# Loading x by eights of batches into a ring of three eights

## What is computed

```python
x = x + einsum('bct,bcd->bdt', x, L0_weights[itok_B_1_198])   # 128 x 128 matrix of 200
x = x + einsum('bct,bcd->bdt', x, L1_weights[itok_B_0_7])     # 128 x 128 matrix of 8
      + bias[itok_B_0_7][:, :, None]
```

## Time and profile before

| | us |
|---|---|
| median of three runs | 342.63 |
| the profiled execution | 343.0 |
| its span, first to last instruction | 341.2 |
| TensorE busy with matmuls | 272.9 (80%) |
| VectorE, ScalarE, GpSimd busy | 126.3, 97.0, 65.8 |
| bytes moved | 140.8 MB, 413 GB/s over the span |
| share of the 16 DMA engines' time, SP's queue | 98.7% |

### The profile page before, as it was taken

How to read it: one execution, slowest core, us unless ns; L and a number is a source line. 1 busy time by engine, 2 the same in 40 slices (tenths; PEclk the granted TensorE clock), 3 DMA queues, 4 the chain that set the end, 5 groups by cost and what they waited for, 6 DMA issues and landing times.

```text
span 341.2 us, 4867 instructions
## 1 busy us (share of the span) xinstructions
PE 272.9 (80%) x774; PEld 131.8 (39%) x774; DVE 126.3 (37%) x202; ACT 97.0 (28%) x135; POOL 65.8 (19%) x249
## 2 busy tenths in 40 slices
PE   1799997678777798786997977889697987978980
PEld 1355443334333354343443433444343443434430
DVE  3145543343333334243442433434243432424440
ACT  1033352232322224132241324313143321323330
POOL 2400311131122211222111222121222111222000
PEclk9999999999999979799897999979799997989996
DMA  7999999999999999999999999999999999999993
GB/s 304 417 409 396 422 430 419 413 423 421 432 434 423 426 422 414 431 424 423 427 427 423 431 430 426 427 421 426 433 426 430 427 429 426 425 426 424 413 387 137
DMA packets 24058, 140.80 MB, mean 413 GB/s; under 512 B 2673, under 2 KB 14322, under 8 KB 15474
## 3 DMA queue, kind: packets, MB, share of 16 engines
q1 hardware_dynamic: 23760, 140.20, 98.7%
q10 hardware_dynamic: 290, 0.53, 0.4%
HBM read 76.03 MB, written 67.11 MB: 419 GB/s over the span
## 4 chain that ended last, share of the span: by engine, by line
DMA 61%; SPq 16%; PE 13%; issue 7%; ACT 0%; DVE 0%; DVEq 0%
DMA out<-xy 54%; PE y_ps L310 11%; SPq L129 9%; SPq L123 5%; DMA xy<-x 4%; DMA w_home<-w_t 2%; PE m_ps L291 2%; SPq L148 2%; ACT xy L406 0%; SPq L162 0%; SPq L151 0%; SPq L203 0%; SPq L156 0%; PE home_ps L324 0%; SPq L176 0%
## 5 line engine op out<-in xcount | busy, mean ns | idle before, releaser
L310 PE MATMUL y_ps<-xy,m_sb 128*128 128x512 f32 x512 | 251.4, 627 | 49.2 <-DMA xy<-x 48.2
L310 PEld LDWEIGHTS y_ps<-xy,m_sb 128*128 128x128 f32 x512 | 94.6, 200 | 155.1 <-issue 155.1
L406 ACT ACTIVATE xy<-y_ps,j_pick 128x512 f32<-128x512 f32 x128 | 88.0, 687 | 227.4 <-PE y_ps L310 227.4
L382 DVE TENSOR_SCALAR xy<-y_ps,j_pick 128x512 f32<-128x512 f32 x128 | 96.1, 751 | 147.9 <-PE y_ps L310 147.9
L242 POOL COPY w_pick<-w_home 128x128 f32 x112 | 33.2, 296 | 238.3 <-issue 238.3
L291 PEld LDWEIGHTS m_ps<-j_pick,w_pick 128*128 128x128 f32 x224 | 35.7, 200 | 30.2 <-issue 29.7
L374 DVE TENSOR_TENSOR m_sb<-m_ps,j_pick 128x256 f32<-128x256 f32 x64 | 27.2, 425 | 47.7 <-PE m_ps L291 46.1
L291 PE MATMUL m_ps<-j_pick,w_pick 128*128 128x128 f32 x224 | 34.9, 279 | 0.0
L244 POOL COPY j_pick<-j_all 128x129 f32 x112 | 33.4, 298 | 0.1
L291 PE MATMUL m_ps<-j_pick,w_home 128*128 128x128 f32 x32 | 5.9, 315 | 6.6 <-DMA w_home<-w_t 6.6
L406 ACT ACT_TABLE_LOAD x7 | 9.0, 1283 | 7.5 <-POOL j_pick L256 7.4
(11 more groups left out here) (16 smaller groups left out, 2.8 us busy)
## 6 DMA issues: line engine op xcount, KB each, us to landing
xy<-x SPq DMA_DIRECT2D x30, 2048.0 KB, 15.1
out<-xy SPq DMA_DIRECT2D x29, 2048.0 KB, 15.0
w_home<-w_t SPq DMA_DIRECT2D x128, 64.0 KB
out<-xy SPq DMA_DIRECT2D x5, 1024.0 KB, 9.7
xy<-x SPq DMA_DIRECT2D x3, 1024.0 KB, 7.7
xy<-x SPq DMA_DIRECT2D x4, 256.0 KB, 13.4
j_all<-w_bias SPq DMA_DIRECT2D x1, 516.0 KB, 3.4
out<-xy SPq DMA_DIRECT2D x2, 256.0 KB, 4.7
```

What stands on the lines that cost most here:

```text
L310: nc.tensor.matmul(y_ps[:, b % YB, h, :], m_sb[:, s, k, :], xy[:, s, k, half(h)], start=True, stop=True).then_inc(y_ready, 1)
L382: nc.vector.tensor_scalar(xy[:, s, k, half(0)], y_ps[:, b % YB, 0, :], j_pick[:, s, k, D:D + 1], None, ALU.add).then_inc(left_out[b % YB], 1)
L406: nc.scalar.activation(xy[:, s, k, half(1)], y_ps[:, b % YB, 1, :], ACT.Identity, bias=j_pick[:, s, k, D:D + 1]).then_inc(right_out[b % YB ...
```

## The change

x (the input alone) is laid out by *eights* of batches: 128 rows of 32 KB, 4.19 MB. `xy` is a ring of three eights (12 pairs instead of 8), and there are five rounds of it and a sixteenth eight at the end. An eight is loaded by one DMA; the first is loaded as two pairs and a quad, the last as a quad, a pair and four halves of a batch. Stores stay quads. `w0_pick`, `j_pick` and `m_sb` shrink to rings of four pairs (PB), and `pick` waits for the results of the pair four behind (`wait_free`), no longer for a store. In SP's order, a step stores a quad, waits for both quads of the eight three behind, loads the eight in its place, and stores the next quad:

```diff
-    RING = 8
...
+    EIGHT = EB // PAIR
+    EIGHTS = 3
+    RING = EIGHTS * EIGHT
...
+    PB = 4
+    BY_PAIR = 3
+    END = EIGHT - 1
...
+            def load_eight(r, e):
+                sp.dma_start(slots(e * EIGHT, EIGHT), eight_of_x(r, e)).then_inc(x_loaded[e], 16)
...
+            def wait_stored(r, e):
+                for q in range(2 * e, 2 * e + 2):
+                    sp.wait_ge(stored[q], stored_once(r, q))
+
+            def next_of(r, e):
+                return (r, e + 1) if e + 1 < EIGHTS else (r + 1, 0)
+
+            def step(r, e):
+
+                behind = next_of(r - 1, e)
+                load_w0_of(r, 2 * e)
+                store_quad(behind[0], 2 * behind[1])
+                load_w0_of(r, 2 * e + 1)
+                wait_stored(r, e)
+                load_eight(r, e)
+                store_quad(behind[0], 2 * behind[1] + 1)
...
             for s in range(QUAD):
-                load_pair(0, s, pair_loaded[s])
+                load_part(0, s, 1, pair_loaded[s])
             sp.wait_ge(cond_loaded, 16)
-            for q in range(QUADS):
-                load_w0_first(q)
-                if q < QUADS - 1:
-                    load_quad(0, q + 1)
+            load_w0_first(0)
+            load_part(0, QUAD, QUAD, quad_loaded)
+            load_w0_first(1)
+            for e in range(1, EIGHTS):
+                load_eight(0, e)
+                load_w0_first(2 * e)
+                load_w0_first(2 * e + 1)
...
             sp.wait_ge(home_ready, 4)
...
+            load_w0_of(1, 0)
+            for s in range(EIGHT):
+                store_pair(0, s)
+            load_w0_of(1, 1)
+            for s in range(EIGHT, EIGHT + QUAD):
+                store_pair(0, s)
+            wait_stored(1, 0)
+            load_eight(1, 0)
             store_quad(0, 3)
...
+            for e in range(1, EIGHTS):
+                step(1, e)
+            with sp.Fori(2, ROUNDS) as r:
+                for e in range(EIGHTS):
+                    step(r, e)
+
...
+            load_w0_of(ROUNDS, 0)
+            store_quad(ROUNDS - 1, 2)
+            load_w0_of(ROUNDS, 1)
+            wait_stored(ROUNDS, 0)
+            load_part(NE - 1, 0, QUAD, last_quad_loaded)
+            load_part(NE - 1, QUAD, 1, last_pair_loaded)
             for k in range(PAIR):
                 for h in range(2):
-                    sp.dma_start(xy[:, LAST, k, half(h)], x[NQ - 1, :, QB - PAIR + k, half(h)])\
+                    sp.dma_start(xy[:, END, k, half(h)], x[NE - 1, :, EB - PAIR + k, half(h)])\
                       .then_inc(last_x_loaded[2 * k + h], 16)
-            for q in range(1, QUADS - 1):
+            for q in range(3, QUADS):
                 store_quad(ROUNDS - 1, q)
-            store_pair(ROUNDS - 1, LAST - 1)
+            store_quad(ROUNDS, 0)
+            store_pair(ROUNDS, END - 1)
...
+            def wait_free(r, s):
+
+                n, behind = (r, s - PB) if s >= PB else (r - 1, s - PB + RING)
+                for k in range(PAIR):
+                    b = behind * PAIR + k
+                    pool.wait_ge(left_out[b % YB], n * (ROUND_B // YB) + (b // YB + 1))
+                    pool.wait_ge(right_out[b % YB], n * (ROUND_B // YB) + (b // YB + 1))
...
-                    pool.wait_ge(stored[s // QUAD], stored_once(r, s // QUAD))
                     pick(r, s)
+            for s in range(EIGHT):
+                pick(ROUNDS, s)
```

More of the change, by code:

```diff
@@ L12, in conditioned_residual_kernel @@
 def conditioned_residual_kernel(nc, x, cond, w0_t, w1_bias, out):
-    NQ, C, QB, T = x.shape
-    B = NQ * QB
+    NE, C, EB, T = x.shape
+    NQ, _, QB, _ = out.shape
+    B = NE * EB
     N0, _, D = w0_t.shape
@@ L145, in load_w0, with load_part @@
                     load_one(b + k, s + k // PAIR, words[2 * k], words[2 * k + 1])
[L147 to L151, removed]
+            def load_part(n, s, pairs, loaded):
+                sp.dma_start(slots(s, pairs), part_of_x(n, s, pairs)).then_inc(loaded, 16)
+            def load_eight(r, e):
+                sp.dma_start(slots(e * EIGHT, EIGHT), eight_of_x(r, e)).then_inc(x_loaded[e], 16)
             def wait_out(r, s):
@@ L193, in _ @@
[L193 to L199, removed]
-            store_quad(0, 3)
[L201 to L209, removed]
@@ L253, in pick_first @@
                     skip_runtime_bounds_check_because="each word is checked against its own range below")
+                if s >= PB:
+                    wait_free(0, s)
                 for k in range(PAIR):
@@ L298, in results @@
                 if k == 0:
-                    if first and s < QUAD:
+                    if last:
+                        if s < QUAD:
+                            pe.wait_ge(last_quad_loaded, 16)
+                        elif s < END:
+                            pe.wait_ge(last_pair_loaded, 16)
+                    elif first and s < QUAD:
                         pe.wait_ge(pair_loaded[s], 16)
-                    elif not last:
-                        pe.wait_ge(x_loaded[s // QUAD], r * 16 + (16 if s >= QUAD else 0))
+                    elif first and s < EIGHT:
+                        pe.wait_ge(quad_loaded, 16)
+                    else:
+                        pe.wait_ge(x_loaded[s // EIGHT], r * 16 + (16 if s >= EIGHT else 0))
                     pe.wait_ge(m_ready[s % MB], r * (RING // MB) + (s // MB + 1))
                 for h in range(2):
-                    if last:
+                    if last and s == END:
                         pe.wait_ge(last_x_loaded[2 * k + h], 16)
@@ L337, in _ @@
                     results(r, s - 1, 1)
+            results(ROUNDS - 1, LAST, 0)
+            product(ROUNDS, 0)
+            results(ROUNDS - 1, LAST, 1)
+            for s in range(1, EIGHT):
+                results(ROUNDS, s - 1, 0, last=True)
+                product(ROUNDS, s)
+                results(ROUNDS, s - 1, 1, last=True)
             for k in range(PAIR):
-                results(ROUNDS - 1, LAST, k, last=True)
+                results(ROUNDS, END, k, last=True)
         @block.vector
@@ L391, in _ @@
                     left(r, s, 1)
[L392 to L395, removed]
-                left(ROUNDS - 1, s, 1)
+            for s in range(EIGHT):
+                left(ROUNDS, s, 0)
+                if s < END:
+                    sum_m(ROUNDS, s + 1)
+                left(ROUNDS, s, 1)
         @block.scalar
```

101 lines of the change are left out of this document (48 added, 53 removed).

## The result

The changed kernel takes 355.06 us (354.21 to 358.53, five runs) beside 342.96 of the kernel before on the same chip: 1.037 of it [1.035, 1.040], 12 us more. The forecast was 342.5, no change, with 345.0 as the upper end.

A forecast was written before the change was run, and what follows sets the result against it. Transfers on full DMA engines, ending with the slowest, were taken to bound the kernel. Terms -1.0 + 0.2 + 0.7 = -0.1 us against the profiled 343.0 us, 0.4 above the median, gave 342.5 us, range 340.3 to 345.0.

The forecast's parts named there:

- What bounds the kernel: Whole kernel: DMA engines are full, the slowest sets the end, and only holes on it cost time.
- Part 1: Large loads of x: 32 KB rows mean fewer packets, 7 to 13 ns saved for each large one; -1.0 us.
- rival C: Loads of x: the chip cuts 32 KB rows into two packets, nothing gained but small packets; 343.4 us, chance 0.10.
- Part 2: Unconditional first round of W0 loads: grows from 16 to 24 batches, one repeated matrix more loaded; +0.2 us.
- Part 3: Start: full queue holds SP at W0 loads behind the third eight, first store late, a hole on all engines; +0.7 us.
- Rival B: Start: queue full before SP's last unconditional W0 loads are in, hole of 3.0 us; 344.8 us, chance 0.14.
- Part 4: Loop: 4.9 us behind the awaited store suffices for the slowest engine; engines ahead may run dry; cost 0.
- My tells: Signs to look for: loop shares a little under 1.00; against it, low shares in every step with TensorE waiting longer.
- `wait_free` and the rings: Picks in the loop: the pair four behind was done some 11 us before it is needed; cost 0.
- Computing stays covered: Loop: TensorE needs 17.5 of 20.6 us for two quads, so computing stays hidden behind transfers; cost 0.
- Rival D: Loads of x: reads spaced by 32 KB are slower, +2.9 us and no packet gain; 346.3 us, chance 0.07.
- Tail: End: three quads' stores (14.7 us) behind the last loads close the hole at 324 us, which was free; cost 0.

The follow-up runs named there:

- e2: Changed kernel with the second store of each step issued before the wait and the load, rows still 32 KB: 348.86 us, 1.019.
- e3: Changed kernel with e2's store order, and each eight loaded by two transfers with rows of 16 KB: 347.60 us, 1.015.
- e6: Kernel before, SP's loop written out, each load also waiting until the previous load landed, so one quad's store (4.9 us) stands behind: 369.06 us, 1.080.
- e8: Kernel before with only the change's small rings of picks and products (four pairs): 343.14 us, 1.0017.
- e5: e3 with a semaphore for each quad of x, so TensorE may start at an eight's first quad: 347.08 us, 1.014.
- e4: Kernel before, own order and ring, with x laid out by eights: 16 KB rows spaced by 32 KB: 342.84 us, 1.0008.
- e10: The control with 32 more waits on a long-reached semaphore in each of SP's unrolled steps: 349.14 us, 1.019.
- e11: Kernel before with 32 more waits on a long-reached semaphore in each step of SP's loop, not unrolled: 343.64 us, 1.003.
- the control: Kernel before with SP's loop only written out (unrolled), no wait added: 344.64 us, 1.007.
- e9: Changed kernel's rings and layout, but each step stores a quad, waits for the quad six behind and loads one quad: 346.75 us, 1.013.

## Why the prediction was wrong

**What bounds the kernel.** Right: the transfers do, before and after. Right too that the end belongs to the slowest engine. Wrong was what I took from it, that only a hole on that engine costs anything.

**Part 1, rows of 32 KB: right in mechanism.** 23760 - 22032 = 1728 packets fewer in SP's queue: 1792 large and 224 small ones less, as forecast, and against them 144 for the W0 load and 144 for a quad that is now stored as two pairs. A 32 KB row is one packet (rival C is out); undisturbed it takes 1213 ns against twice 611, 9 ns saved, where I took 7 to 13. But the microsecond never reached the time, since slow packets cover it; and where part of these were gone, in e2 and e3, the kernel with large rows was the longer one by 1.3 us.

**Part 2, one more W0 load: right**, 0.06 MB more.

**Part 3, the start: right in mechanism, too large in size.** SP was held by the full queue as described (after, start us, us, line, transfers):

```profile
16.93 6.05 SPq L165 DMA_DIRECT2D xy<-x  x1
23.48 13.80 SPq L143 DMA_DIRECT2D w_home<-w_t  x12
37.47 3.09 SPq L180 DMA_DIRECT2D out<-xy  x4
```

All twelve W0 loads, however, were in the queue (23.48 + 13.80 = 37.3 us) before the last engine was through with the third eight, at 38.1 us, and the store came at once. I had put two or so of them behind that moment. The windows there:

```profile
36.00:37.00 1.00, 1.00 (x6) 0.60 (x5) 0.42 (x1) 0.66 (x1) 0.07 (x1) 1.00 0.44 137
37.00:38.00 1.00, 1.00 (x4) 0.44 (x3) 0.72 (x1) 0.00 (x0) 0.00 (x0) 1.00 1.15 300
```

0.4 us at most, against 0.7. Rival B, 3.0 us, is out.

**Part 4, the loop: this is the step that failed.** I wrote that 4.9 - 2.2 "leaves at least 2.7 us on the slowest engine, so nothing is lost there. Engines that are up to 5 us ahead of it do run dry, and can afford it". The 5 us between the engines were right, and the 2.7 us were near (by the trace 3.2 to 4.1). What is false is that nothing is lost and that the engines ahead can afford it. With 4.9 us behind the awaited store the packets of a load take up to 3.1 us instead of 1.2, behind its start on the engines that ran dry, and at its end on all 16, so that the slowest engine is held too. The idle time itself is small, some 2 us for each engine over the whole run; the slow packets are some 15 us. The price of this term was 0; e6 gives it by itself as 1.0 us a step, so 12 us.

My tells failed with it. I looked for "shares of a little under 1.00", and for "low shares in every step" as the sign against me. Shares stay at 1.00, because a slow packet counts as busy. GB/s is the column that falls. Two other signs were there: TensorE waited longer (48.2 us before, 53.7 after), and the last engine stood 2 us nearer to the first (a lag of 3.6 us at 300 us, 5.8 before). The prediction's last words even name the fault, that 4.9 us is too little to stand behind the store, but gave it neither a price nor a chance.

**`wait_free` and the rings: right** within 0.6 us (e8). **Computing stays covered:** not quite. As long as a full eight must land, results are late enough to empty a longer queue (e3 has slow packets in the loop, e5 none).

**Rival D, the spacing: out** (e4, 1.0008). The rule of the Trainium skill beside it (DMA: Bandwidth & Descriptors, Latency and other measured facts) speaks of pitches from 512 KiB up; 32 KB here cost nothing, and no run here shows a larger one.

**Tail.** As forecast there is no hole at 324 us (1.01, 389 GB/s), and that was worth nothing.

**The sum.** -1.0 + 0.2 + 0.0 to 0.4 for the first three parts, of which the -1.0 is not seen in any time, and 12 us for the fourth. No rival held it: each rival was a price of a part in which I saw a cost, and part 4 had been closed at 0.

**What stays open.** That the short queue costs the 12 us is shown: e6 makes the same loss for each step in the kernel before, by it alone, and e2, e3 and e5 take it away in the loop, step by step. Why packets are slow then was not found; the trace shows when and on how many engines, not what they wait for. That engines which ran dry start together is not enough to explain it: slow packets also come at the ends of loads, and at loads for which no engine had run dry (51 and 94 us after, 238 to 250 us in e10). The missing proof is a run in which only some of the engines restart. That instruction packets set the last engine back is shown by the steps in e10, e11 and the control. They don't account for all of e9's 4.3 us: its packets at 69.9, 98.4, 114.5 and 151.0 us come with steps of 0.4, 0.1, 0.6 and 1.0 us, the large one at 86.2 us with none, and the rest of its lag grows between packets, twice as fast as before (0.2 and 0.1 us in 10). The cause of that is open. In e5 the lag grows as far, to 8.9 us at 298 us, so a part of its 4.5 us can be the same and not the tail.

## What to carry to other kernels

Where a DMA queue bounds a kernel, compare what stands behind the awaited transfer with the distance between the first and the last of the 16 engines plus the start of a load; where it was shorter, each step cost about 1 us on all engines, although none of them seemed idle. Making the transfer twice as large, without putting more behind the awaited store, halved this reserve here, from 9.8 to 4.9 us. Read GB/s beside the share: a busy share of 1.00 says nothing of how fast the packets go.

## What the runs showed of the hardware

- A short queue costs more than the idle time in it: 1.0 us a step with 4.9 us behind the awaited store, nothing measurable with 9.8 us as long as the lag stayed under 7.6 us, at busy shares of 1.00 and 1.01. The idle time was 2 us for each engine in the changed kernel, the slow packets 15 us.
- One DMA engine falls behind steadily, to 6.8 us before and to 10.2 us in e9. It falls behind by 0.1 to 0.2 us in 10 without any visible cause, and at packets of instructions (8 KB, 0.31 us) by 0.4 to 1.2 us in e10, 0.5 to 0.9 in its control. Unrolling SP's loop alone cost 2.1 us (344.64 against 342.55). The Trainium skill (DMA: Bandwidth & Descriptors, Latency and other measured facts) knows two engines that are usually slower, and names as a guess the rings of descriptors that GpSimd's transfers use; here no such transfer was issued, one engine is late (in e9 5.6 us behind the last but one at 302 us), and the steps come with the instruction packets.
- One transfer's issue can hold SP for 6.05 us when the queue is full.
